# Lists built sooner, weight fetches in another order, and the pairs' output biases spread by TensorE from eight rows

## The reference, cut to what matters

```python
# layer 0 experts: top 2 of 8, gated two-layer net of width 352
x = x + L0_ffn(_layernorm(x), wqkv, w1, w2)
# layer 1: graph part + linear attention, layernorm
xn = _layernorm(x)
x = x + L1_gnn(xn, W, a, src, dst) + L1_mix(xn, W_Q, W_K, W_V, W_fc, gamma, beta)
# layer 1 experts: the one best of 8, width 512, with biases
feats = _layernorm(x)
eid = argmax(feats @ centroids.T)
for e in range(8):
    h = xhat * gamma[e] + beta[e]
    y = feats + relu(h @ w1[e] + b1[e]) @ w2[e] + b2[e]
    alpha = sigmoid(feats @ centroids[e])
    out += mask_e * (alpha * y + (1 - alpha) * feats)
```

## Time and profile before

| | us |
|---|---|
| median of 3 runs (1037.71 to 1039.08) | 1037.92 |
| the profiled execution's own time | 1036.91 |
| its span, first to last instruction | 1035.1 |
| TensorE busy | 1003.3 (97%) |
| VectorE / GpSimd / ScalarE busy | 370.0 / 315.8 / 203.6 |
| 16 DMA engines, mean rate over the span | 167 GB/s |

### The profile page before, as it was taken

The page is one execution under the profiler, slowest core; times in us unless marked ns, Lnnn a source line. Parts: engine busy times, 40 slices in busy tenths (PEclk is TensorE's granted clock), DMA queues, the critical chain, the costliest instruction groups (busy, mean ns, idle before and its releaser), DMA issues.

```text
span 1035.1 us, 10355 instructions
## 1 busy us (share of the span) xinstructions
PE 1003.3 (97%) x3570; PEld 537.3 (52%) x3570; DVE 370.0 (36%) x1025; ACT 203.6 (20%) x416; POOL 315.8 (31%) x245
## 2 busy tenths in 40 slices
PE   5999999999999999999998999999999999998997
PEld 4555555555555544544556665534444455455322
DVE  6034573046200055830246101054103057567314
ACT  3123221111111126830021111111002010012400
POOL 2787787878888840000000000010000000000310
PEclk9999999999999999999999999999999999999999
DMA  9755545453544461013147888780632215636996
GB/s 326 196 102 143 141 102 142 108 136 82 143 102 102 105 225 47 1 41 102 41 133 274 297 330 349 266 304 41 203 101 102 81 42 187 259 128 230 374 362 247
DMA packets 63565, 173.29 MB, mean 167 GB/s; under 512 B 22192, under 2 KB 22928, under 8 KB 63392
## 3 DMA queue, kind: packets, MB, share of 16 engines
q1 hardware_dynamic: 38800, 146.56, 41.7%
q0 software_dynamic: 20672, 14.58, 8.2%
q10 hardware_dynamic: 4048, 11.59, 3.1%
HBM read 160.74 MB, written 11.95 MB: 167 GB/s over the span
## 4 chain that ended last, share of the span: by engine, by line
PE 82%; DMA 9%; DVE 3%; issue 3%; ACT 1%; SPq 1%; POOL 0%; ACTq 0%; DVEq 0%; POOLq 0%
PE bank L1056 36%; PE bank L1067 16%; PE bank L1043 9%; PE bank L1304 6%; PE bank L1329 3%; PE bank L1514 3%; DMA rows<-in_stream 2%; DMA Y<-in_stream 2%; PE bank L1157 2%; PE bank L1469 2%; DMA G<-in_stream 1%; DMA Y<-xs,idx 1%; PE bank L1143 1%; SPq L534 1%; PE bank L1288 1%
## 5 line engine op out<-in xcount | busy, mean ns | idle before, releaser
L1056 PE MATMUL bank<-xnT,ring 128*128 128x384 f32 x896 | 292.4, 487 | 1.2 <-ACT xnT L718 1.2
L1056 PEld LDWEIGHTS bank<-xnT,ring 128*128 128x128 f32 x896 | 169.6, 190 | 121.7 <-issue 3.6
L551 POOL DMA_INDIRECT n_lo<-count,ridx x48 | 83.3, 1735 | 17.3 <-issue 14.0
L551 POOL DMA_INDIRECT n_hi<-count,ridx x48 | 80.9, 1685 | 17.1 <-issue 13.7
L605 POOL DMA_INDIRECT Y<-xs,idx x8 | 7.6, 956 | 251.6 <-DVE idx L2050 178.9
L1067 PE MATMUL bank<-ring,Y 128*128 128x512 f32 x192 | 83.9, 595 | 0.0
L1067 PE MATMUL bank<-ring,xnT 128*128 128x512 f32 x192 | 82.7, 592 | 0.0
L1056 PE MATMUL bank<-Y,ring 128*128 x256 | 82.7, 486 | 0.0
L605 POOL DMA_INDIRECT G<-xs,idx x2 | 1.9, 951 | 249.1 <-DMA xs<-Y 245.4
L1304 PE MATMUL bank<-ring,Y 128*128 128x352 f32 x256 | 77.8, 461 | 0.0
L742 ACT ACTIVATE Y<-bank,sbias,scale 128x384 f32 (+1 forms) x48 | 32.2, 670 | 202.3 <-PE bank L1056 202.3
(11 more groups left out here) (354 smaller groups left out, 1112.0 us busy)
## 6 DMA issues: line engine op xcount, KB each, us to landing
ring<-in_stream SPq DMA_DIRECT2D x144, 512.0 KB, 3.8
ring<-in_up SPq DMA_DIRECT2D x32, 704.0 KB, 6.2
Y<-in_stream SPq DMA_DIRECT2D x18, 512.0 KB, 8.0
G<-in_stream SPq DMA_DIRECT2D x16, 512.0 KB, 10.2
ring<-in_dn SPq DMA_DIRECT2D x7, 1024.0 KB, 5.9
rows<-keys SPq DMA_DIRECT2D x10, 512.0 KB
ys<-Y ACTq DMA_DIRECT2D x9, 512.0 KB, 7.8
xnT<-in_stream SPq DMA_DIRECT2D x6, 512.0 KB, 10.5
```

Source lines behind the costliest of these rows:

```text
L551: pool.indirect_dma_start(table, bass.IndirectOffsetOnAxis(ap=at[:, e:e + 1], axis=0), what[:, e:e + 1], None, **how).then_inc(done, 16)
L1056: last = pe.matmul(bank[to][:, 0:N], ring[:, r, k * P:(k + 1) * P], rhs(k), start=(k == 0), stop=(k == KB - 1))
```

## The change

1. **Routing of layer 0.** DVE makes the one-hot matrices of experts 1 to 3 only, waits for their list, copies it, and then makes those of 4 to 7. TensorE lists 1 to 3 ahead of the first `up` and 4 to 7 ahead of its third quarter. SP issues the `up` loads of expert 1 ahead of expert 7's `down` weights.
2. **End of layer 0 experts.** Expert 7's `down` goes to banks 0 and 1, ahead of the two late sums of expert 6, and no longer waits for `y_done`.
3. **Start of layer 1.** Block 0 is normalised in two halves, its first half transposed and evicted at once, and two of its slots multiplied before the second half is there.
4. **Pairs.** `list_pairs` waits for nothing of ACT's. `turn_pair_rows(1)` comes behind the whole of `up_pair(0)`, `turn_pair_rows(2)` behind `up_pair(1)`. DVE does `v_rows_T(0)` first, and `normalise_features` behind the scores; `v_hidden` of pair 0 comes ahead of `v_rows_T(1)`.
5. **Fetches.** Six loads of pair 1's second weights (r = 1, 5, 2 and 6, 3, 7) now wait for `xs_stored`; before, the first three waited only for the affinities, and the last three for `odd_gathered`.
6. **Biases.** All eight `b2` rows are loaded once (32 KB) into `b2all`; each `down_pair` begins with four products of a repeated column of the identity (8 by 64) with `b2all` (L1635 of the changed kernel). DVE copies in place of adding.

```diff
-        last_sums = [bank[i] for i in (2, 3, 4, 1, 6, 7)]
+        last_sums = [bank[i] for i in range(2, 8)]
...
+        b2all = Y[0:NE, 5, 2048:3072]
...
+            def next_up(e):
+                for j in range(4):
+                    sp.wait_ge(M0.up_used, 4 * e - 3 + j)
+                    load_up(e, j)
+
+            next_up(1)
             sp.wait_ge(x1_done, 6)
             sp.dma_start(G[:, 6144:8192].rearrange("p (k n) -> p k n", k=2),
                          dn0_d[NE - 1, 0:2 * P, :].rearrange("(k p) n -> p k n", p=P)).then_inc(dn_last, 16)
             sp.dma_start(dnb_over, dn0_d[NE - 1, 2 * P:F0, :]).then_inc(dn_last, 16)
-
...
-            next_up(1)
...
-            def load_b2(i):
-                for a in range(2):
-                    sp.dma_start(b2row[a * HC:(a + 1) * HC, :], b2_d[2 * i + a].to_broadcast([HC, D]))\
-                        .then_inc(b2_in, 16)
...
-            load_b2(0)
+            sp.dma_start(b2all, b2_d.rearrange("e o d -> (e o) d")).then_inc(b2_in, 16)
...
             sp.wait_ge(pe_output, AFF2)
+            sp.wait_ge(xs_stored, 32 * NB)
             for r in (1, 5, 2):
                 load_w2(1, r)
             sp.wait_ge(M1s.xt_ready, 2)
-            sp.wait_ge(odd_gathered, 16)
             for r in (6, 3, 7):
                 load_w2(1, r)
...
-                    act.activation(Xg[:, half * 512:(half + 1) * 512], bank[5 + half][:], ACT.Copy).then_inc(S.y_done, 1)
+                    act.activation(Xg[:, half * 512:(half + 1) * 512], bank[half][:], ACT.Copy).then_inc(S.y_done, 1)
...
-                    if i == 0 and k == 1:
+                    if i < 2 and k == 1:
                         last.then_inc(t_evicted, 1)
...
-            def next_b2(i):
-
-                act.wait_ge(M1s.y_done, i)
-                for a in range(2):
-                    act.dma_start(b2row[a * HC:(a + 1) * HC, :], b2_d[2 * i + a].to_broadcast([HC, D]))\
-                        .then_inc(b2_in, 16)
...
             def turn_block(base, normed_before, b):
 
-                pe.wait_ge(xn_ready, normed_before + b + 1)
                 for i in range(2):
+                    if i or b or base != T_LN3:
+                        pe.wait_ge(xn_ready, normed_before + b + 1)
                     pe.wait_ge(t_evicted, base + 2 * b + i - 1)
...
             def first_up_arrived(j):
                 if j == 0:
-                    pe.wait_ge(R0.slots, 3)
-                elif j < 3:
-                    list_rows(*((1, 4), (4, NE))[j - 1])
+                    list_rows(1, 4)
+                if j == 2:
+                    list_rows(4, NE)
...
                 turn_hidden(S, NE - 1, kind)
+                down_(NE - 1)
                 pe.wait_ge(M0.y_done, NE - 1)
                 for half in range(2):
                     pe.matmul(last_sums[3 * half][:], late_T[:, 3 * P:4 * P], Yb[:, half * 512:(half + 1) * 512],
                               start=True, stop=False, skip_group_check=True)
-                down_(NE - 1)
...
-                    down(M0, e, 0, G, dnb_over, lambda j: pe.wait_ge(dn_last, 32), True, True)
+                    down(M0, e, 0, G, dnb_over, lambda j: pe.wait_ge(dn_last, 32), False, True, 0)
...
+            pe.wait_ge(gates_ready, 2)
             turn_block(T_LN3, 2 * NB, 0)
             for b in range(NB):
+                if b == 0:
+                    pe.wait_ge(t_evicted, T_LN3 + 1)
+                    block_rows(0, range(0, 2), xtok, arr(0)(0), True, False, 0)
                 pe.wait_ge(t_evicted, T_LN3 + 2 * b + 2)
                 for half in range(2):
-                    block_rows(b, range(4 * half, 4 * half + 4), xtok, arr(0)(half), True, True, half)
+                    first = 2 if b == 0 and half == 0 else 4 * half
+                    block_rows(b, range(first, 4 * half + 4), xtok, arr(0)(half), first % 4 == 0, True, half)
                     if b == 0:
...
-                    if i == 0 and j == 0:
-                        pe.wait_ge(t_evicted, T_FE + 2 * NB + 1)
-                        list_pairs()
-                    elif j == (i == 0):
+                    if i < 2 and j == 0:
+                        pe.wait_ge(t_evicted, T_FE + 2 * NB + 1 + i)
+                    elif j == (i < 2):
                         pe.wait_ge(M1s.xt_done, i + 1)
                     if j == 2:
                         pe.wait_ge(upper_done, i + 1)
-                    if i == 0 and j == 3:
-                        turn_pair_rows(1)
...
                     pe.wait_ge(M1s.y_done, i)
                 else:
                     pe.wait_ge(upper_done, 3)
+                pe.wait_ge(b2_in, 16)
+                for half in range(2):
+                    for a in range(2):
+                        pe.matmul(bank[5 + half][a * HC:(a + 1) * HC, :],
+                                  ident[0:NE, 2 * i + a:2 * i + a + 1].to_broadcast([NE, HC]),
+                                  b2all[:, half * 512:(half + 1) * 512], start=True, stop=False, skip_group_check=True)
...
-                                                 start=(kk == 0 and k == 0), stop=(kk == 1 and k == 1),
+                                                 start=False, stop=(kk == 1 and k == 1),
...
+            list_pairs()
             for i in range(PAIRS):
                 up_pair(i)
-                if i:
+                if i == 0:
+                    turn_pair_rows(1)
+                    turn_slots()
+                else:
+                    if i == 1:
+                        turn_pair_rows(2)
                     down_pair(i - 1)
-                if i + 2 < PAIRS:
-                    turn_pair_rows(i + 2)
-                if i == 0:
-                    turn_slots()
+                    if i == 1:
+                        turn_pair_rows(3)
                 turn_hidden(M1s, i, 1)
...
-                for e in range(1, NE):
+                for e in range(1, 4):
                     one_hot_slots(e, posm).then_inc(R.slots, 1)
                 v.wait_ge(R.listed, 1)
                 v.tensor_copy(idx[:, 1:4], bank[1][:, 1:4]).then_inc(R.rows_known, 1)
+                for e in range(4, NE):
+                    one_hot_slots(e, posm).then_inc(R.slots, 1)
...
-                    last = tt(Yb[:, o], bank[5 + half][:], b2row[:, o], ALU.add)
+                    if arrived:
+                        last = tt(Yb[:, o], bank[5 + half][:], b2row[:, o], ALU.add)
+                    else:
+                        last = v.tensor_copy(Yb[:, o], bank[5 + half][:])
...
-                b2_arrived(PAIRS - 1)
                 for half in range(2):
                     v.wait_ge(M1s.dn_used, 4 * PAIRS - 1 + half)
                     o = slice(half * 512, (half + 1) * 512)
-                    tt(Xg[:, o], bank[5 + half][:], b2row[:, o], ALU.add).then_inc(M1s.y_done, 1)
+                    v.tensor_copy(Xg[:, o], bank[5 + half][:]).then_inc(M1s.y_done, 1)
...
+                if b == 0:
+                    for half, done in ((0, gates_ready), (1, xn_ready)):
+                        o = slice(half * 512, (half + 1) * 512)
+                        ts(xn[:, b, o], xr[:, b, o], mv[:, b, 0:1], rstd[:, b:b + 1], ALU.subtract, ALU.mult).then_inc(done, 1)
+                else:
+                    normalise_block(xn, xr, b, xn_ready)
...
             route_pairs()
-            for b in range(NB):
-                normalise_features(b)
+            v_rows_T(0)
             step(tt(gat, small(120, 24), aff, ALU.mult))
             step(v.tensor_reduce(small(204, 3), gat3, AX.X, ALU.add))
             tt(small(24, 3), small(204, 3), root, ALU.mult).then_inc(act_input, 1)
-            v_rows_T(0)
             v.wait_ge(act_output, AF)
             scores(R1, [oh1], [m1], HC, hbase)
+            for b in range(NB):
+                normalise_features(b)
+            v_hidden(M1s, 0, 1, step)
             v_rows_T(1)
-            v_hidden(M1s, 0, 1, step)
```

24 lines of the change are left out of this document (10 added, 14 removed).

## The result

| | before | changed |
|---|---|---|
| median (4 runs each) | 1038.04 us | 1046.91 us (1045.34 to 1047.78) |
| ratio, 95% interval | | 1.0089 (1.0074 to 1.0103) |
| profiled span | 1035.1 | 1043.4 |
| TensorE busy | 1003.3 | 1015.0 |

The change made the kernel 8.9 us slower, by the medians, and 8.3 by the two profiled spans. The prediction was 1038.1 with 1041.3 as its upper end, so it was wrong. The largest single miss belongs to rival 4, a lower clock of TensorE behind the new wait: 3.3 us, where the sum had nothing and the rival 1.5 to 2.5. It is less than half of the 8.1 us by which the profiled spans miss the forecast; the gains of part 1 and of the start of the pairs came out 2.0 short each.

A forecast was written before the change was run, and what follows sets the result against it. TensorE was taken as the bound, busy 1003.3 of 1035.1 us. Terms -2.8 + 0 - 2.7 + 0.9 + 2.2 + 8.0 - 5.5 + 0.1 = +0.2 gave 1037.1 profiled, 1038.1 median; range 1034.5 to 1041.3.

The forecast's parts named there:

- rival 4: Idle 2.2 us ahead of down_pair(0) lowers TensorE's clock: +1.5 to +2.5, 1039.6 to 1040.6; chance 0.15.
- the start of the pairs: up_pair(1) starts near 960.9, pair 1's gather taking 8.1 us and TensorE waiting 1.9: -2.7, bounds -4.6 and -0.9.
- part 1's 2.8: Layer 0 routing: expert 1's gather no longer awaited, up(1) starts near 563.3 instead of 566.16: -2.8 us.
- Parts 2 and 3: 0: End of the experts and start of layer 1: no gain, with 1.0 us gained as the bound.
- +0.9: turn_pair_rows(2) moves from ahead of up_pair(1) to behind it: +0.9 us.
- +2.2: TensorE idles ahead of down_pair(0) for DVE's eight scalings of pair 2's rows: +2.2 us, bounds 2.1 and 3.7.
- +8.0: Sixteen bias products, 2.0 us a pair: +8.0; bounds 6.9 and 13.8 + 1.2.
- the 0.3 in it: Going to the bias products' tile form and back: 0.3 us a pair, on top of 1.72 for the columns.
- rival 3: Bias products of the two halves run one behind the other: +6.9 us, 1045.0; chance 0.10.
- -5.5: Weight stalls in down(2) and down(3), put on repeated bias row transfers, go: -5.5 us, bounds -2.9 and -5.5.
- +2.5 net: Part 6 as a whole: +8.0 us for the bias products against -5.5 for the stalls.

The follow-up runs named there:

- run 6: Part 1 alone on the kernel before: 1035.21 us beside 1037.67, ratio 0.9981.
- run 9: Run 7 plus sixteen small thrown-away fp16 products in the wait for pair 1's gather: 1033.55 us beside 1037.15, ratio 0.9975.
- run 1: Changed kernel with turn_pair_rows(2) moved behind the second quarter of up_pair(1): 1039.46 us beside 1037.69, ratio 1.0024.
- run 2: Changed kernel with twelve small thrown-away fp16 products filling the wait ahead of down_pair(0): 1042.74 us beside 1037.69, ratio 1.0059.
- run 3: Changed kernel with the last three loads of pair 1's second weights held until pair 1's gather landed: 1043.42 us beside 1037.69, ratio 1.0054.
- run 4: Changed kernel with part 6 undone (old bias transfers and adds back): 1036.57 us beside 1037.69, ratio 0.9993.
- run 5: Part 6 alone on the kernel before: 1040.52 us beside 1037.67, ratio 1.0030.
- run 7: Changed kernel with part 6 undone and turn_pair_rows(2) behind the second quarter of up_pair(1): 1033.84 us beside 1037.67, ratio 0.9971.
- run 11: Run 1 plus turn_slots inside up_pair(0) and pair 0's bias products in the wait for pair 1's gather: 1037.46 us beside 1037.15, ratio 1.0007.
- run 12: Run 7 with part 5 undone too, so parts 1 to 4 with the turn put back: 1035.86 us beside 1037.52, ratio 0.9989.
- run 8: Run 7 with all six loads of pair 1's second weights held until pair 1's gather landed: 1040.13 us beside 1037.67, ratio 1.0017.
- run 10: Kernel before with part 1, and last three loads of pair 1's second weights released by the xs store's landing: 1036.41 us beside 1037.15, ratio 0.9993.

## Why the prediction was wrong, by its steps

**What failed.** The sum left out the lower clock behind the wait that the change itself puts ahead of `down_pair(0)`: 3.3 us. It carried part 1's 2.8 undiminished to the pairs, where 1.0 arrived, and it had `up_pair(1)` start 2.5 nearer to `up_pair(0)`, where 0.5 came.

**Part 1 was right where it was worked out and wrong in what was carried on.** `up(1)` starts at 563.33 (forecast 563.3) with 0.98 of waiting for DVE ahead of the hidden rows. The -2.83 is -2.05 at the turn of expert 3's rows (580.60, before 582.65), whose gather is now awaited for 0.84. It took 5.9 from its issue at 574.58, before 4.9; expert 7's 1.4 MB had landed by 571.69, so whether they delay it is not shown. At block 2 of layer 1 the gain is 708.21 - 706.59 = 1.6, and at `up_pair(0)` 1.0: ten small products at 942 took 3.31 for 1.78, with the granted clock at 0.50, the 1.2 GHz level, until 945.7. Alone the part is worth 2.0 to 2.5 (run 6).

**Parts 2 and 3: 0, in line with the forecast.** From `up(1)` to block 2's turn it takes 143.26, and 142.95 with part 1 alone (before 142.05); the 0.3 between the first two is within what executions differ by. They were not run by themselves.

**The start of the pairs was mis-sized.** Nothing held the half. ACT's last store of `xs` released SP's loads 4.1 after its issue (945.30 to 949.37), for the 2.9 that I took from the earlier trace rows; the gather was issued at 950.07 and took 8.93 (forecast 8.1, bounds 4.6 and 9.9), so the wait was 2.76 for 1.9. The transposes, slots and hidden rows behind it took 3.09 for my 2.0, at the lower clock; run 9 has them at 2.08. I had argued from the 1.76 wait of the earlier trace rows, which left the clock alone, and treated it as evidence about longer ones.

**`turn_pair_rows(2)`: +0.9 and +2.2, both right** (0.93 and 2.25), and the step that failed is the next: what this idle time does to the clock. I put +1.5 to +2.5 on it as rival 4, at 0.15, and nothing in the sum. It was 1.54 on the bias products (3.40 for 1.86) and 1.80 on `down_pair(0)` (8.82 for the 7.02 that it takes at the full clock behind a bias group), +3.3. Runs 1 and 2 show it from both sides: take the wait away and 6.7 go by the medians, 5.0 in that stretch; keep the wait and fill it and 3.1 go, 3.34 in that stretch. My price came from one place, 561 to 566, where eight transposes and little else fell into the slow time; here a bias group and a large part of a `down_pair` did. Runs 3 and 4, at 1.7, lie in rival 4's range, so the 3.3 is what this execution paid, and not a constant.

**Biases: +8.0 was right, and the 0.3 in it too.** A group takes 1.86 from its start to that of the next product, but the change of form also costs something in the products round it. From `up_pair(3)` to the hidden rows behind `down_pair(2)`, in the changed kernel and in run 4, which has no bias products and no stall there:

```profile
1002.93 7.09 PE L1619 MATMUL bank<-ring,Y 128*64 128x512 f32 x32
1018.83 0.66 PE L1300 MATMUL bank<-k,Y 128*128 128x128 f32 x4
...
996.94 7.09 PE L1633 MATMUL bank<-ring,Y 128*64 128x512 f32 x32
1010.82 0.66 PE L1314 MATMUL bank<-k,Y 128*128 128x128 f32 x4
```

15.90 less 13.88 is 2.02, which is 1.72 for the columns and 0.30 for going there and back. Some of that is luck: the 0.24 that I leaned on was read to a modelled end, and to the start of the next row (869.93) the group of the earlier trace rows is only 0.16 above its columns. The last group, behind `spread`, costs 1.86 (8.88 less 7.02), so the four come to 7.9. The two halves overlap, so rival 3 is wrong. The Trainium skill, TensorEngine Tiling (Array Packing), section Tiling Modes, says that a change of the tiling mode drains TensorE; the 0.30 agrees with it, and no run separates a drain from other costs of the change.

**-5.5 for the stalls was right, its reason was half of the matter.** Measured against 13.88 and 7.02, the kernel before loses 2.2 on `down_pair(2)` and 3.0 on `down_pair(3)`, 5.3. I put it all on the repeated rows. Without them the loads land in time (run 5), but with them and sooner requests only 1.6 is left (run 7). In the sum it makes no difference; as a judgement of part 6 it does: I had the part at +2.5 net, which is right on the kernel before (+2.9, run 5), and it costs 7.9 and its share of the lower clock where part 5 has already taken away most of the stalls.

**The sum by measured terms** of the profiled executions: -1.0 to `up_pair(0)`, -0.5 to `up_pair(1)`, then +0.4 (`up_pair(1)`, 7.34 for 6.92, in part at the lower clock), +1.1 (the turn), +2.25, +3.4 and +1.85 (`down_pair(0)`, 8.82 for 6.97), which are the third line's 9.0, and +0.6 and +0.2: 8.3.

## What to carry to other kernels

A wait of two us ahead of a long run of products can cost more than itself: here the lower clock added 1.7 to 3.3 behind 2.25 us of waiting. Price it with the products that follow it at half clock, as the unfavourable bound, and fill it with work that is due anyway (run 11's bias group was free there) or put the work that makes the wait among products (run 1). Two edits that end the same stall are not paid twice: judge each with the other in place. A stall that is gone proves little when the engine also came later: compare the landings, or two runs in which it came at the same time (runs 7 and 9 against the kernel before and run 12). Where the DMA engines are full from one point to the last load, a load held back for a gather was a weight late at the end here (runs 8, 10 and 12 moved waits from one place to the other and won nothing).

## What the runs showed that I had not expected

- The 2.25 of idle time in the changed kernel lowered the clock for about 7 us: `down_pair(0)`'s first products came 0.85 to 0.90 apart in place of 0.43 until about 980. In run 3, behind 2.24 of idle time, the first 2.8 us of products ran at the full clock and the lower one came after them.
- Behind gather waits of 2.2 to 3.5 the lower clock added about 1.1 to 1.3 (runs 1, 3, 4 and 7 and the changed kernel); behind single waits of 1.76 (before), 1.5 (run 9) and 0.95 (run 12) the transposes took their 1.09 to 1.10.
- Ten 128x384 fp16 products behind eight 128x8 fp32 ones took 1.78 or 1.79 in some executions (before, runs 3, 5, 9 and 11) and 2.95 to 3.36 in the others, at a granted clock of 0.50 in the changed kernel, with nothing waiting. What decides it stays open; run 3 and the changed kernel have the same program there.
- Runs of one kernel lie up to 6 us apart (the kernel before 1034.09 to 1039.89 in 31 runs), so that a term below 2 us is only to be had from ten runs, or from neighbouring marks of a trace.
